# A quantised weight product folded into a feed-forward layer, on one core: other groups of weight tiles, and another spread of the quantising

## What is computed

```python
# weight, W_base: 2048 x 2048; x: 32 x 128 rows of 2048; 16 groups of 128 inputs
lora_delta = lora_B @ lora_A * 0.5
cb = codebook / max(abs(codebook))                  # 32 levels
scale = exp(scale_log)
normalized = (weight + lora_delta).reshape(O, 16, 128) / scale
thresholds = (cb[:-1] + cb[1:]) * 0.5               # 31 of them
quantized = cb[searchsorted(thresholds, normalized, side='left')]
w_eff = (quantized * scale).reshape(O, I) + lora_delta
c = x @ w_eff.T
result = c @ W_base.T + b_base
ax, probs = c @ A_w.T, softmax(c @ router_w.T)
mixed = einsum(einsum(ax, cores), probs)            # 8 experts, rank 16
out = x + result + 2 * mixed @ B_w.T
```

## Time and profile before

| | us |
|---|---|
| median of 3 executions | 2498.99 |
| lowest, highest | 2495.66, 2500.41 |
| profiled execution, its own time | 2502.43 |
| its span in the profile | 2500.6 |
| mean granted clock of TensorE | 0.987 of full |
| PE busy | 2373.2 (95%) |
| DVE busy | 1795.6 (72%) |
| ACT busy | 1499.5 (60%) |
| POOL busy | 1203.9 (48%) |

### The profile page before, as it was taken

How to read it: one execution, slowest core, us unless ns; L and a number is a source line. 1 busy time by engine, 2 the same in 40 slices (tenths; PEclk the granted TensorE clock), 3 DMA queues, 4 the chain that set the end, 5 groups by cost and what they waited for, 6 DMA issues and landing times.

```text
span 2500.6 us, 31530 instructions
## 1 busy us (share of the span) xinstructions
PE 2373.2 (95%) x11808; PEld 2129.7 (85%) x11808; DVE 1795.6 (72%) x2274; ACT 1499.5 (60%) x1906; POOL 1203.9 (48%) x742
## 2 busy tenths in 40 slices
PE   5688998899999999999999999999999999999999
PEld 2345777787988899999999999899999989899998
DVE  5898998698899987858878858866666634344444
ACT  5898999677788857657666636654544414311111
POOL 3677877544688763436776633444554310010010
PEclk9999999999999999999999999999999999999999
DMA  4565556544788773345666643446665544456665
GB/s 157 184 231 182 206 201 214 183 141 143 250 288 294 286 257 115 114 135 211 238 227 231 226 169 103 119 143 218 223 238 212 211 142 131 140 215 234 237 239 199
DMA packets 141981, 493.06 MB, mean 197 GB/s; under 512 B 15058, under 2 KB 75986, under 8 KB 100818
## 3 DMA queue, kind: packets, MB, share of 16 engines
q1 hardware_dynamic: 141828, 491.05, 56.8%
HBM read 305.91 MB, written 185.07 MB: 196 GB/s over the span
## 4 chain that ended last, share of the span: by engine, by line
PE 77%; DVE 11%; ACT 5%; issue 2%; POOL 2%; DMA 2%; SPq 0%; DVEq 0%; POOLq 0%; ACTq 0%
PE m L621 17%; PE m L622 17%; PE m L623 17%; DVE acc L879 9%; PE m L605 8%; PE m L606 8%; PE m L607 8%; PE pd L559 2%; ACT mk L739 2%; PE m L651 1%; DMA part<-part 1%; ACT mp L749 1%; POOL pp L1024 1%; ACT ds L727 1%; DVE kl L906 1%
## 5 line engine op out<-in xcount | busy, mean ns | idle before, releaser
L879 DVE SCALAR_TENSOR_TENSOR acc<-mk,dj,acc 128x1024 f32<-128x1024 uint8 x800 | 1025.1, 1281 | 117.8 <-ACT mk L739 53.6
L739 ACT ACTIVATE mk<-wr,bj 128x1024 uint8<-128x1024 f32 x800 | 902.6, 1143 | 232.7 <-DVE acc L879 222.5
L621 PE MATMUL m<-gh,xh 128*128 128x384 f32 (+2 forms) x2560 | 913.7, 357 | 25.6 <-DVE part L896 11.3
L622 PE MATMUL m<-gl,xh 128*128 128x384 f32 (+2 forms) x2560 | 902.6, 353 | 0.0
L623 PE MATMUL m<-gh,xl 128*128 128x384 f32 (+2 forms) x2560 | 900.3, 352 | 0.0
L621 PEld LDWEIGHTS m<-gh,xh 128*128 128x128 f32 x2560 | 484.2, 189 | 84.2 <-issue 24.7
L623 PEld LDWEIGHTS m<-gh,xl 128*128 128x128 f32 x2560 | 483.7, 189 | 23.4
L622 PEld LDWEIGHTS m<-gl,xh 128*128 128x128 f32 x2560 | 484.8, 189 | 20.6
L1020 POOL TENSOR_SCALAR tm<-mp,dj 128x1024 f32<-128x1024 uint8 x192 | 218.3, 1137 | 452.6 <-ACT mp L749 448.3
L901 DVE TENSOR_TENSOR part<-m,part 128x384 f32<-128x384 f32 (+2 forms) x480 | 280.2, 585 | 215.3 <-PE m L623 214.8
L605 PE MATMUL m<-kh,wh 128*128 128x384 f32 (+2 forms) x1120 | 398.6, 356 | 25.6 <-DVE kl L906 17.4
(11 more groups left out here) (88 smaller groups left out, 1439.1 us busy)
## 6 DMA issues: line engine op xcount, KB each, us to landing
part<-part SPq DMA_DIRECT2D x256, 1036.0 KB, 4.8
kw<-in_wb SPq DMA_DIRECT2D x192, 192.0 KB, 2.4
rows<-in_wb SPq DMA_DIRECT2D x32, 1036.0 KB, 4.8
out<-part SPq DMA_DIRECT2D x32, 1024.0 KB, 4.0
wr<-in_w SPq DMA_DIRECT2D x32, 512.0 KB, 5.9
kw<-in_wb SPq DMA_DIRECT2D x64, 256.0 KB, 2.6
xw<-in_x SPq DMA_DIRECT2D x64, 256.0 KB, 3.1
dl<-delta SPq DMA_DIRECT2D x30, 512.0 KB, 5.8
```

Source lines behind the costliest of these rows:

```text
L621: e.matmul(R.m[c][:, 0:w], xh, gh, start=k == 0, stop=False)
L622: e.matmul(R.m[c][:, 0:w], xh, gl, start=False, stop=False)
L739: e.activation(R.mk[k % NM], w, ACT.Identity, bias=R.bj[:, j:j + 1], scale=GROW).then_inc(S["mk"], 1)
L879: e.scalar_tensor_tensor(R.acc, R.mk[k % NM], R.dj[:, j:j + 1], R.acc, ALU.mult, ALU.add).then_inc(S["ac"], 1)
```

## The change

Groups become (3, 3, 3, 3, 4). POOL sums seven levels (NP = 7), DVE 24, with new places for the spare levels, `normalise` after level 8 and `split` at level 11. The quantising is written as one running `Background` with a target half for the end of every stage (UNTIL_TOKENS, UNTIL_WEIGHTS), shared out evenly within a stage: 7 halves at the start-up, then 6 (tokens of group 0), 2, 4, 2, 4, 2, 5 (tokens of group 3), none. Splits are made as soon as the half is quantised and its high buffer is free, so those of the next group no longer stand at the end of a token stage (but for the very last). In the first two halves behind the start-up, deltas stand at every third level (eight in a half), later four in a half. The load of partial sums for token t + 1 is asked for at chunk 0 of token t, ahead of the store of t - 1, in place of t + 2 at chunk 3.

```diff
@@ -23,22 +23,24 @@
 DX = D + XW
 NC = 32
 NJ = NC - 1
-NP = 6
+NP = 7
 NV = NJ - NP
-SPARE_AT = (0, 3, 9, 13, 17, 21)
+SPARE_AT = (0, 3, 6, 10, 13, 16, 19)
+NORM_AT, SPLIT_AT = 8, 11
 CUT = (0, 384, 768, 1152, 1664, DX)
 NCH = 5
 GROW = float(2.0 ** 100)
 FULL = 255.0
 
-GROUP = (2, 3, 4, 4, 3)
+GROUP = (3, 3, 3, 3, 4)
 NG = len(GROUP)
 FIRST = tuple(sum(GROUP[:g]) for g in range(NG + 1))
 GC_BEFORE = tuple(NCH * sum(n - 1 for n in GROUP[1:max(g, 1)]) for g in range(NG))
 LAST = NG - 1
 N0 = GROUP[0]
 NMAX = max(GROUP)
-LOOK0, LOOK = 1, 2
+LOOK0 = 1
+UNTIL_TOKENS, UNTIL_WEIGHTS = (13, 19, 25, 32), (0, 15, 21, 27, 32)
 RAW = 2 * NMAX + 3
 HIGH = 2 * NMAX
 NM = 3
@@ -71,15 +73,6 @@
     return next(g for g in range(NG) if FIRST[g] <= b < FIRST[g + 1])
 
 
-def units(q):
-
-    for j in range(NV):
-        yield ("unit", q, j)
-        if j == 8 and q not in (2 * b for b in FIRST):
-            yield ("split", q - 1)
-    yield ("effect", q)
-
-
 def startup():
     for q in range(2 * N0 + LOOK0):
         for j in range(NV):
@@ -94,33 +87,58 @@
     yield ("rows_out", N0 - 1)
 
 
-def weights_of(g, ahead):
-
-    late = [ev for ev in ahead if ev[0] == "split"]
-    ahead = [ev for ev in ahead if ev[0] != "split"]
-    done = 0
+class Background:
+
+
+    def __init__(self):
+        self.q, self.j, self.split = 2 * N0 + LOOK0, 0, 2 * N0
+
+    def level(self, consumed):
+        yield ("unit", self.q, self.j)
+        if self.j == SPLIT_AT:
+            yield from self.splits(self.q, consumed)
+        self.j += 1
+        if self.j == NV:
+            yield ("effect", self.q)
+            self.q, self.j = self.q + 1, 0
+
+    def splits(self, until, consumed):
+        while self.split < until and self.split - HIGH < consumed:
+            yield ("split", self.split)
+            self.split += 1
+
+    def levels(self, until, share, consumed):
+
+        left = NV * (until - self.q) - self.j
+        for _ in range(max(0, left - int(self.total * (1 - share)))):
+            yield from self.level(consumed)
+
+    def begin(self, until):
+        self.total = NV * (until - self.q) - self.j
+
+
+def weights_of(g, back):
+
+    until = UNTIL_WEIGHTS[g]
+    back.begin(until)
     for s in range(NS):
         yield ("slot", g, s)
         if s % NB == NB - 1:
             yield ("chunk_out", g, s // NB)
         if s == NS - 10:
             yield ("x_first", g)
-        goal = max(done, min(len(ahead), len(ahead) * (s + 1) // (NS - 6)))
-        yield from ahead[done:goal]
-        done = goal
-    yield from late
-
-
-def tokens_of(g, rest):
-
-    done = 0
+        yield from back.levels(until, min(1.0, (s + 1) / (NS - 6)), 2 * FIRST[g])
+
+
+def tokens_of(g, back):
+
+    until = UNTIL_TOKENS[g]
+    back.begin(until)
     for t in range(NT):
         for c in range(NCH):
             yield ("chunk", g, t, c)
-            goal = max(done, min(len(rest), len(rest) * (NCH * t + c + 1) // (NT * NCH - 10)))
-            yield from rest[done:goal]
-            done = goal
-    yield ("split", 2 * FIRST[g + 2] - 1)
+            yield from back.levels(until, min(1.0, (NCH * t + c + 1) / (NT * NCH - 10)), 2 * FIRST[g + 1])
+    yield from back.splits(2 * FIRST[g + 2], 2 * FIRST[g + 1])
     yield ("close", g)
 
 
@@ -145,13 +163,12 @@
 def walk():
 
     yield from startup()
-    ready = 2 * N0 + LOOK0
+    back = Background()
     for g in range(NG):
         if g:
-            ready = 2 * FIRST[g + 1] + (LOOK if g < LAST else 0)
-            yield from weights_of(g, [ev for q in range(2 * FIRST[g + 1], ready) for ev in units(q)])
+            yield from weights_of(g, back)
         if g < LAST:
-            yield from tokens_of(g, [ev for q in range(ready, 2 * FIRST[g + 2]) for ev in units(q)])
+            yield from tokens_of(g, back)
     yield from last_tokens()
 
 
@@ -277,7 +294,8 @@
 
     places = {(0, 1): ("direct", 2), (0, 3): ("direct", 3)}
     places.update({(0, 5 + n): ("delta", n) for n in range(16)})
-    late = [(q, j) for q in range(2 * N0 + 1, NQ) for j in (3, 9, 15, 21)]
+    busy = 2 * N0 + 1
+    late = [(q, j) for q in range(busy, NQ) for j in (range(1, NV, 3) if q <= busy + 1 else (3, 9, 15, 21))]
     places.update({at: ("delta", 16 + n) for n, at in zip(range(NDELTA - 16), late)})
     return places
 
@@ -504,10 +522,10 @@
             if c == 0:
                 if t + 2 < NT:
                     load_x(g, t + 2)
+                if g and 2 <= t < NT - 1:
+                    load_part(g, t + 1)
                 if t:
                     store_part(g, t - 1)
-            if c == 3 and g and t and t + 2 < NT:
-                load_part(g, t + 2)
             if t == NT - 1 and c == 1:
                 for s in range(4):
                     weight(g + 1, s)
@@ -1057,7 +1075,7 @@
             q, j = at
             if j in SPARE_AT:
                 spare(q, SPARE_AT.index(j))
-            if j == 9 and q + 1 < NQ:
+            if j == NORM_AT and q + 1 < NQ:
                 normalise(q + 1)
         elif what == "effect":
             effective(*at)
```

## The result

| | before | changed |
|---|---|---|
| median, us | 2499.7 (4 executions) | 2598.8 (4 executions, 2594.2 to 2601.9) |
| profiled execution | 2502.4 | 2594.2 |
| span | 2500.6 | 2592.4 |

The ratio is 1.0396, with a 95% interval of 1.0374 to 1.0418: 99 us slower. No change was forecast: 2502 us, in a range of 2486 to 2516.

What follows compares the result with a forecast made beforehand. TensorE was taken to bound the token stages, with idle time in group 0. Start-up, token and weight terms summed to +3.6 us on the profiled 2502.43; less 3.4 to the median, 2503, rounded down to 2502, range 2486 to 2516.

Steps and rivals of the forecast that it cites:

- the one on the partial sums: Token stages: asking for the load of partial sums one token ahead costs nothing; its cover is one token, 8.5 us.
- late partial sums: Rival, token stages: load and store outlast a token, DVE waits; 0.3 us on some 90 tokens, 2530 us; chance 0.04.
- Term 151.0: Weight stages of groups 2 and 3, 3 tiles in place of 4: 151.0 us each against 186.9.
- group 1's 159.0: Weights of group 1, same 3 tiles and two halves: 159 us, +0.8, with 154 and 164 as ends.
- by the weight stages: Slower rival: DVE, not TensorE, ends slots of 3-tile weight stages with quantising; 2514 to 2525 us; chance 0.26.
- The seventh level was booked at nothing: Weight stages of groups 2 and 3: +2.9 us on kl, 2 x 1.28 taken from DVE; nothing won.
- The term for kl beside POOL: Weight stages: 25.8 us of DVE time in kl hang on POOL's work; two more levels there add 2.9.
- closing writes 36.0 apart: Start-up, seven half tiles in place of five: POOL bounds a half at 36.0 us; stage 301.5 us, +69.0.
- the tokens of group 0: Three tiles, 32 deltas, six halves quantised beside TensorE, all fitting: 313.3 us, +66.1, bounds 310 and 325.
- the price of a tile in tokens and of the deltas: Token stages: 90.6 us a tile; 1.25 us per 512-column delta, at most 1.07 per 384-wide one.
- the last two stages: Weights of group 4, +43.2 to 189.4 us; last tokens, 4 tiles, +90.6 to 414.3 us.
- The rival in which the levels too are held by POOL: Port lock shared by DVE and POOL also delays DVE's levels (L879): +16, 2518 us; chance 0.02.

Runs made afterwards that it cites:

- the groups alone: Kernel before with groups 3, 3, 3, 3, 4 and the delta places they need, old load, six POOL levels: 2572.8 us, 1.0288.
- The half moved away: Changed kernel, store issued before load, one half tile moved from weight stages of groups 2 and 3 to token stages of groups 1 and 2: 2495.6 us.

## Why the prediction was wrong

**The step that failed** is the one on the partial sums: "I book nothing. The cover is one token, 8.5 us". I looked at when a load is asked for, and compared it with the time of one load. "No longer behind the wait for the store of t-1" is true, but the load of t + 1 waits for the store of t - 2 instead, and I did not follow what queues behind that wait on SyncE: the store of t - 1, on whose landing the next load depends. What was put at nothing is a floor of 9.1 us or more per token. The three token stages sum to 900.4 us with the load first and 820.7 with the store first: 80 us hang on the order of two issues. The rival "late partial sums" had the right place and the sign by which it would show, but no circle, 0.04 of chance and a third of the price: 0.3 us a token, where it is 0.8 (76 us over 96 tokens).

**Its evidence was misread.** "The 3-tile stage carried 281 GB/s" was true of a stage whose tokens lasted 9.2 us, 20 deltas among them, with load and store by turns. Shortening the token to 8.4 us and putting both in flight together are not covered by that row, and the runs with the old place of the load (2596.2 us, and two held stages with the groups alone) show that shorter tokens alone are enough. So the new place of the load did not cause the loss by itself: the changed kernel would have been held with the old one too.

**Weight stages.** Term 151.0 measured 158.8 and 160.0, group 1's 159.0 measured 162.3. The rival "by the weight stages" (157 each, 165 for group 1) described it: in group 2's the wait for kl was 10.8 with one of 6.3 us at the start, that for gl 5.8, 16.6 in all, where I had booked 5.5 and 6.3. The half moved away shows that the quantising ended the slots. The groups alone, with six levels and the old spread, took 151.3 and 151.7 us there, near the term; but 1.9 and 7.9 us of waiting for POOL's last split stand just before those two stages, so this does not tell how much the spread adds. The seventh level was booked at nothing there, and with the store first it costs 1.4 and 4.5 us. The term for kl beside POOL was close; DVE's busy time in kl (L924), weights of groups 2 and 4:

```profile
1077.20:1236.00 158.80, 78.03 (x78) 0.97 0.45 138
...
1994.90:2181.60 186.70, 45.98 (x78) 0.99 0.38 110
```

78.03 us less the 45.98 of group 4's stage, where POOL is busy 3.04 us, are 32.1; expected were 25.8 + 2.9 = 28.7. The profile has POOL busy 80.46 us there, not the 73.6 that two more levels make of 66.46.

**Right by their own steps:** the start-up (301.4, closing writes 36.0 apart, so that 1.2 of the 1.39 us come in); the tokens of group 0, where TensorE is busy 312.00 of 312.0 us, so that the idle time of before is gone; the price of a tile in tokens and of the deltas; the last two stages within 3.5. The last split of the last group, which still stands at a stage's end, cost more than the nothing I gave it: PE waited there for POOL in the changed kernel

```profile
PE m L623 <- POOL wl L1053: 7.8, 1, 7.8
```

which lies in the 301.2 us of group 3's tokens. With the store first that stage has 2.3 us of idle time in all. The whole of the rest, +3.6 us forecast, is +10.9 with the store first (span 2511.5 against 2500.6): the same sign, and mis-sized by the weight stages.

The rival in which the levels too are held by POOL did not come: 768 levels took 1270 to 1292 ns, with POOL busy 1317 us in place of 1204.

## What to carry to other kernels

When a DMA is moved in an in-order queue, list what then stands behind its wait, and ask whether that wait depends on one of them: a load that waits for a store, with the next store queued behind it, makes a circle that turns once in the landing time of that store, with the load's bytes in flight beside it. Here a stage hid the circle as long as its own period was longer, so check it again whenever the period shrinks, and issue what releases buffers first. And when work moves into smaller stages, compare the helper's time in each with the stage's own new length, not with a sum over the kernel.

## What the runs showed of the hardware

With a 1 MB load and a 1 MB store behind it by 0.5 us, the load took 6.5 us in the median to land and the store 8.6; with the store 0.4 us ahead of the load, the store took 5.0 and the load 7.8; where they went by turns, 4.8 each over the kernel. In these runs what was issued second paid for the overlap. A 192 KB transfer issued behind the pair took 8.3 us, and 3.1 us when issued ahead of it. Turning two lines of a queue changed nothing in bytes and 85 us in time. The kernel's 3-tile token stages carried 279 to 282 GB/s with the store first and 252 to 257 in the circle, at the same DMA share (0.78 to 0.79): the same bytes in more time, so the lower rate is the effect, not the cause. A DVE subtraction of two SBUF tensors took 1.00 us on average in a stage where POOL was busy half of the time (78.03 us for 78), and 0.59 where POOL was nearly idle (45.98 for 78); a mask times step plus accumulator did not slow at all.
